# Attention over eight elements: scattered operand loads by groups of four heads, Q and K projected early, row maxima spread from the first score on

## The reference, cut to what matters

```
x: (8, 256, 512)   cond: (8, 512), zeros and ones
# layer 0: attention along the last axis, 16 heads of 16, masked
Q, K, V = W @ x[b]                         # 256x256 weights, 512 tokens
att = softmax((Q K^T / 4 + b0) * m + (1 - m) * -1e30)
x = x + (att V)^T
# layer 1: attention over 256 tokens, 16 heads of 32
xn = rms_norm(x) * g * (1 + scale) + shift # scale, shift from cond
q, k, v = xn @ W_qkv;  q, k = rms_norm(q), rms_norm(k)
o = softmax(q k^T / sqrt(32)) v
x = x + o + o @ W_out
# layer 2: a GRU over 256 steps.  layer 3: block attention and layer norm
```

## Time and profile before

| what | value |
|---|---|
| median of three runs | 2219.55 us |
| the profiled execution, its own time | 2220.39 us |
| its span in the trace | 2218.5 us |
| mean granted TensorE clock | 0.861 of full |
| busy: PE, DVE, ACT, POOL | 1912.1, 1271.6, 1088.1, 375.9 us |
| attention, until the GRU's first matmul | 0 to 1227.65 us |

### The profile page before, as it was taken

One profiled execution on the slowest core, in us unless ns is written; L12 is line 12 of the kernel. 1 busy time (PEld: TensorE's weight loads), 2 busy tenths in 40 slices (PEclk: granted clock), 3 DMA queues, 4 the chain that ended last, 5 costly groups with the idle time before them and its releaser, 6 DMA issues. The chain is left out here.

```text
span 2218.5 us, 87931 instructions
## 1 busy us (share of the span) xinstructions
PE 1912.1 (86%) x33566; PEld 1397.6 (63%) x33566; DVE 1271.6 (57%) x5543; ACT 1088.1 (49%) x4105; POOL 375.9 (17%) x1398
## 2 busy tenths in 40 slices
PE   5857978898788887898997899999999998989876
PEld 3224445363454544545463788888888898989775
DVE  4526346274462743636423477777777777777766
ACT  0332634635436354372653455555556565656444
POOL 3000000000000000000000133333333333343334
PEclk7678989999899999999998879897979797979557
DMA  8041233403333033331212300000000000000002
GB/s 222 6 65 40 61 49 81 68 11 86 54 81 62 9 94 54 81 54 15 72 63 57 101 1 1 0 0 0 0 0 0 0 0 0 0 0 0 0 0 76
DMA packets 100390, 86.87 MB, mean 39 GB/s; under 512 B 12472, under 2 KB 87352, under 8 KB 100296
## 3 DMA queue, kind: packets, MB, share of 16 engines
q1 hardware_dynamic: 99272, 85.41, 17.4%
q10 hardware_dynamic: 640, 0.13, 0.0%
q0 software_dynamic: 384, 0.01, 0.0%
HBM read 60.20 MB, written 21.00 MB: 37 GB/s over the span
## 5 line engine op out<-in xcount | busy, mean ns | idle before, releaser
L1202 PE MATMUL bank_pair_A<-moving,rep 128*128 128x16 f16 x8192 | 328.7, 172 | 69.4 <-ACT bank_pair_C L1285 40.6
L1202 PEld LDWEIGHTS bank_pair_A<-moving,rep 128*128 128x128 f16 x8192 | 268.2, 99 | 107.8 <-DVE moving L1427 81.0
L1202 PE MATMUL bank_pair_C<-moving,rep 128*128 128x16 f16 x8192 | 321.6, 171 | 0.0
L1202 PE MATMUL bank_pair_B<-moving,rep 128*128 128x16 f16 x8192 | 321.6, 171 | 0.0
L1202 PEld LDWEIGHTS bank_pair_B<-moving,rep 128*128 128x128 f16 x8192 | 266.2, 99 | 0.0
L1202 PEld LDWEIGHTS bank_pair_C<-moving,rep 128*128 128x128 f16 x8192 | 266.1, 99 | 0.0
L1294 ACT ACTIVATE r_gate<-r_pre 128x8 f32<-128x8 f32 (+1 forms) x512 | 110.3, 215 | 292.4 <-DVE r_pre L1387 255.2
L1189 PE MATMUL bank_pair_D<-x_part,w_in 128*128 128x256 f16 x1536 | 207.2, 282 | 6.1 <-ACT gi_rz L1322 3.5
L1082 POOL TENSOR_TENSOR x<-x,w_in 128x512 f32<-128x512 f32 x8 | 10.2, 1273 | 1077.8 <-DMA w_in<-w_in 1077.8
L547 PE MATMUL bank_pair_A<-rep 96*128 96x512 f16 x256 | 91.1, 443 | 108.0 <-DMA rep<-parts 65.3
L989 DVE TENSOR_REDUCE head_max<-bank_pair_A 128x2 f32<-128x1024 f32 x128 | 155.9, 1218 | 43.9 <-PE bank_pair_A L547 43.3
(11 more groups left out here) (250 smaller groups left out, 3570.4 us busy)
## 6 DMA issues: line engine op xcount, KB each, us to landing
rep<-parts SPq DMA_DIRECT2D x64, 256.0 KB, 10.9
parts<-parts SPq DMA_DIRECT2D x48, 256.0 KB, 2.1
q_rep<-parts SPq DMA_DIRECT2D x32, 256.0 KB, 4.9
k_rep<-parts SPq DMA_DIRECT2D x64, 128.0 KB, 2.8
w_in<-in_x_dram SPq DMA_DIRECT2D x8, 512.0 KB, 5.2
x<-in_x_dram SPq DMA_DIRECT2D x8, 512.0 KB, 4.4
w_in<-w_in SPq DMA_DIRECT2D x128, 32.0 KB, 2.0
parts<-parts SPq DMA_DIRECT2D x32, 128.0 KB, 2.7
```

The lines of the kernel that those rows point to most:

```text
L1202: last = nc.tensor.matmul(ps[part][:, o:o + 2 * B], w[:, k, (first + c) * P:(first + c) * P + P], moving[:, k, :, :].rearrange("p s b -> p ...
```

## The change

- `load_rep` takes a group of four heads: one DMA of mask rows and eight of 64 KB into the four heads' part of `rep`. The group of element b+1 waits for the last scores of the same group in attend(b), and not for all 32 units. The first maximum of each group waits for that group's loads.
- In attend, `q` moves to units 1 to 4, `k` to 7 to 10, `v0` to 27 to 30; `max1` moves to units 13 to 20 and `neg1`, `row1` to 22.
- Finish begins with a `max`, has one ahead of every `score1`, two behind every `res` and one behind each of the first `qk` chunks; `neg` follows the last of them and `row` the next chunk. Element 0's finish begins with six.
- SP's order: both stores of parts follow the loads of x and the mask; `load_rep` of groups 0 to 3 is placed among three `move_y`. The fourth `move_y` is issued by ACT, ahead of its steps of finish.
- `score1` of heads 0 and 1 share one bank of pair C (head 1 waits for head 0's exponent), then the two banks of pair C take turns.

The diff, cut:

```diff
-        score1_bank = [pA[:, 0, :], pA[:, 1, :], pB[:, 0, :], pB[:, 1, :]] + [pC[:, h % 2, :] for h in range(4, H)]
+        score1_bank = [pC[:, 0, :]] + [pC[:, (h + 1) % 2, :] for h in range(1, H)]
...
+            if b + 1 < B:
+                for n in range(NC * NC):
+                    at(1 + n, ("q", n))
+                at(5, ("q_split", 0))
+                for n in range(NC * NC):
+                    at(7 + n, ("k", n))
+                at(10, ("k_full", 0))
+                at(12, ("k_split", 0))
+                for n in range(DC):
+                    at(27 + n, ("v0", n))
             if b >= 1:
                 for h in range(H):
-                    at(3 + h // 2, ("max1", h))
-                at(11, ("neg1", 0), ("row1", 0))
-            if b + 1 < B:
-                for n in range(NC * NC):
-                    at(14 + n, ("q", n))
-                at(17, ("q_split", 0))
-                for n in range(NC * NC):
-                    at(20 + n, ("k", n))
-                at(23, ("k_full", 0))
-                at(25, ("k_split", 0))
-                for n in range(DC):
-                    at(26 + n, ("v0", n))
+                    at(13 + h // 2, ("max1", h))
+                at(22, ("neg1", 0), ("row1", 0))
...
             for h in range(H):
+                yield from maxes(1)
                 yield "score1", h
...
-                if h >= 8:
-                    yield from maxes(1)
...
+            yield from maxes(1)
             yield "inv1", G - 2
...
-            yield from maxes(1)
             for oc in range(DC):
                 yield "res", oc
-                yield from maxes(1)
+                yield from maxes(2)
                 if oc == 0:
                     yield "xnT", 0
             yield "xT", 0
-            yield from rest_order(free, 2)
+            yield from rest_order(free, 1)
 
         def first_order():
 
             free = iter(range(U0))
+            for u in islice(free, 6):
+                yield "max", u
             yield "x1", 0
             yield "rms", 0
-            yield "norm", 0
             for u in islice(free, 4):
                 yield "max", u
+            yield "norm", 0
             yield "tokens", 0
             yield "xnT", 0
             yield from rest_order(free, 3)
 
         def rest_order(free, per_chunk):
+            done = False
             for m in range(M8):
                 yield "qk", m
-                for u in islice(free, per_chunk):
-                    yield "max", u
+                some = [("max", u) for u in islice(free, per_chunk)]
+                yield from some
+                if some and some[-1][1] == U0 - 1:
+                    yield "neg", 0
+                    done = True
+                elif done:
+                    yield "row", 0
+                    done = False
             yield "qk", M8
-            left = list(free)
-            for u in left:
-                yield "max", u
-            if left:
-                yield "neg", 0
-            yield "v", 0
-            if left:
+            if done:
                 yield "row", 0
-            for n in range(1, DC * NC):
-                yield "v", n
+            yield from (("v", n) for n in range(DC * NC))
...
-            def load_rep(b):
-
+            def load_rep(b, g):
+
+                heads = slice(4 * g, 4 * g + 4)
                 if b >= 1:
-                    sp.wait_ge(st_ps, b * U0)
-                sp.dma_start(k_rep[64:67, :, :], mask_rows[b:b + 1, :, :].rearrange("o r t -> (o r) t").unsqueeze(1)
-                             .broadcast_to([3, H, D])).then_inc(ld_rows, 16)
+                    sp.wait_ge(st_ps, (b - 1) * U0 + 2 * DC * (g + 1))
+                sp.dma_start(k_rep[64:67, heads, :], mask_rows[b:b + 1, :, :].rearrange("o r t -> (o r) t").unsqueeze(1)
+                             .broadcast_to([3, 4, D])).then_inc(ld_rep[g], 16)
                 sp.wait_ge(st_parts, b * 64 + 64)
                 for rep0, rows in ((q_rep, ((0, 0), (0, 32), (1, 16), (1, 48))), (k_rep, ((2, 0), (2, 16), (3, 32), (3, 48)))):
                     for n, row in rows:
-                        sp.dma_start(rep0[row:row + DH0, :, :], parts0[n].rearrange("h d t -> d h t")).then_inc(ld_rep, 16)
-
+                        sp.dma_start(rep0[row:row + DH0, heads, :], parts0[n][heads, :, :].rearrange("h d t -> d h t")).then_inc(ld_rep[g], 16)
...
-                move_y(b, 0)
                 if more:
                     store_parts(b + 1, 0)
-                move_y(b, 1)
+                    store_parts(b + 1, 1)
+                for g in range(G - 1):
+                    if more and g >= 1:
+                        load_rep(b + 1, g)
+                    move_y(b, g)
+                    if more and g == 0:
+                        load_rep(b + 1, g)
                 if more:
-                    store_parts(b + 1, 1)
-                move_y(b, 2)
-                if more:
-                    load_rep(b + 1)
+                    load_rep(b + 1, G - 1)
                 else:
                     sp.wait_ge(st_ps, B * U0)
                     sp.dma_start(w_ih_f32, W_ih.rearrange("(c p) n -> p c n", p=P)).then_inc(w_ih_ld, 16)
-                move_y(b, 3)
                 spread1(b)
...
-                        pe.wait_ge(max1_ok, b - 1)
+                        pe.wait_ge(v1_ok, b - 1)
...
+                if tc == 0 and b >= 2:
+                    pe.wait_ge(max1_ok, b - 1)
...
-                if u == 0:
-                    pe.wait_ge(ld_rep, b * 128 + 128)
-                    pe.wait_ge(ld_rows, b * 16 + 16)
-                    pe.wait_ge(q_lo_ok, b + 1)
-                if u == 1:
-                    pe.wait_ge(kf_ok, b + 1)
+                if u % (2 * DC) == 0:
+                    pe.wait_ge(ld_rep[u // (2 * DC)], b * 144 + 144)
+                if b == 0 and u == 0:
+                    pe.wait_ge(q_lo_ok, 1)
+                if b == 0 and u == 1:
+                    pe.wait_ge(kf_ok, 1)
                 if u < 2:
-                    if b >= 2:
-                        pe.wait_ge(exp1_ok, (b - 2) * H + 2 * u + 2)
-                    elif b == 1:
-                        pe.wait_ge(exp_ok, U0)
+                    if b >= 1:
+                        pe.wait_ge(exp_ok, b * U0 - 1 + u)
                 else:
                     pe.wait_ge(s_max, b * U0 + (u - 1))
...
                 if h == 0:
                     pe.wait_ge(max1_ok, e + 1)
-                if e + 1 < B:
-                    if h in (0, 2):
-                        pe.wait_ge(exp_ok, (e + 2) * U0 - 1 + h // 2)
-                    if h in (4, 5):
-                        pe.wait_ge(y_ok, (e + 1) * G + (h - 1))
-                elif h == 4:
-                    pe.wait_ge(qn_ok, e * M8 + M8)
-                if h >= 6:
+                if h == 0:
+                    if e + 1 < B:
+                        pe.wait_ge(y_ok, (e + 1) * G + 3)
+                    else:
+                        pe.wait_ge(qn_ok, e * M8 + M8)
+                elif h == 1:
+                    pe.wait_ge(exp1_ok, e * H + 1)
+                elif h == 2 and e + 1 < B:
+                    pe.wait_ge(y_ok, (e + 1) * G + 4)
+                elif h >= 3:
                     pe.wait_ge(exp1_ok, e * H + (h - 1))
...
+            def move_last_y(b):
+
+                g = G - 1
+                act.wait_ge(y_ok, b * G + G)
+                for j in range(4):
+                    r = (4 * g + j) * DH0
+                    act.dma_start(y[r % P:r % P + DH0, r // P, :], y_pad[g % 2][32 * j:32 * j + DH0, :]).then_inc(ld_y[g % 2], 16)
...
                 if b + 1 < B:
                     v_part(b + 1)
+                move_last_y(b)
                 steps(BESIDE[b], b, b - 1)
```

More of the change, by code:

```diff
@@ L250, in _ @@
                 last.then_inc(c_condt, 1)
-        ld_x1, ld_mask, ld_rows, st_parts, ld_rep, ld_max = (
-            sem(n) for n in ("ld_x1", "ld_mask", "ld_rows", "st_parts", "ld_rep", "ld_max"))
+        ld_x1, ld_mask, st_parts, ld_max = (sem(n) for n in ("ld_x1", "ld_mask", "st_parts", "ld_max"))
+        ld_rep = [sem(f"ld_rep_g{g}") for g in range(G)]
         ld_y = [sem(f"ld_y{n}") for n in range(2)]
@@ L408, in _, with move_y @@
         def _(sp):
+            def move_y(b, g):
+                sp.wait_ge(y_ok, b * G + g + 1)
+                for j in range(4):
+                    r = (4 * g + j) * DH0
+                    sp.dma_start(y[r % P:r % P + DH0, r // P, :], y_pad[g % 2][32 * j:32 * j + DH0, :]).then_inc(ld_y[g % 2], 16)
             def load_x(b):
@@ L427, in store_parts @@
                 if b >= 1:
-                    sp.wait_ge(ld_rep, b * 128)
+                    for g in range(G):
+                        sp.wait_ge(ld_rep[g], b * 144)
                 for n, ready in ((0, q_hi_ok), (1, q_lo_ok)) if which == 0 else ((2, k_hi_ok), (3, k_lo_ok)):
@@ L472, in _ @@
             store_parts(0, 1)
-            load_rep(0)
+            for g in range(G):
+                load_rep(0, g)
```

(2 more changed lines are left out.)

## The result

| | before | after |
|---|---|---|
| median, us | 2219.55 (2216.96 to 2224.35, 11 runs) | 2227.04 (2221.09 to 2232.15, 11 runs) |
| the profiled execution, its own time / span | 2220.39 / 2218.5 | 2232.15 / 2230.3 |

The ratio is 1.003, with a 95% interval of 1.0018 to 1.0041: slightly slower, where 2180 was forecast. The profiled execution lies 5.1 above its median. Part of that can be its launch: its first maximum comes at 35.95, and in eight other profiled executions with the same start (experiments 1 to 3, 5 to 7, 9 and 10) it comes at 32.7 to 33.5 in five and at 35.4 to 35.9 in three. Against the profiled execution of before, the first eight matmuls of the Q projection ran at half clock (6.67 us for the group that took 3.67 there) and began 0.8 later.

What follows compares the result with a forecast made beforehand. Attend was taken as bound by PE, finish by waits for `rep` and DVE's maxima. Terms -12.5 - 18.4 - 71.1 + 7.3 + 54 + 1.2 = -39.5 took 2220.4 to 2180.9, so 2180; range 2148 to 2214.

Steps and rivals of the forecast that it cites:

- the wait for x: At attend's Q projection: x lands at A (start of the next attend) + 10.8, so PE stands about 10 us.
- The issues on ACT: At finish's start: ACT's four DMAs for the last `y` take 2.4 us ahead of its first exponent.
- PE's restart: After the second `score1`'s wait: PE restarts about T (end of attend's last `pv`) + 6.1; half clock adds 1.7.
- the `qk` chunks: In finish: chunks fall from 3.5 to 2.6 and 2.2 us; first `qk` to A takes 30.2.
- x does stop PE: Denies the rival of no stop: `spread1` pieces keep pace with PE, 61 us stay saved, 2119; chance 0.07.
- ACT's issues: Rival at finish's start: the four issues take 7.4, 5 us more in seven finishes, 2215; chance 0.07.
- the last of them: Rival: group loads wait in SP's queue, PE still waits 7.9 for `rep`, about 2227; chance 0.05.
- clock rival: Rival: clock stays at half through finish's `score1` stretch, 12 us an element, +72, 2252; chance 0.07.
- Attend becomes 10.8 + (49.6 - 0.9) + 0.2 for `q_split` ... + 2.5: Attends 2 to 6: x's landing, PE's remaining work, `q_split` and clock restart make 62.2, 10.8 more each.
- 15.8 ... 2.2 ... 1.7 ... T + 25.8 at the third `weigh1`: Finish's score stretch: 14 maxima 15.8, DVE's other steps 2.2, half-clock restart 1.7; third `weigh1` at T + 25.8.
- First maximum near 31: Kernel start: only a quarter of `rep`'s bytes is needed, first maximum at 31.3, saving 12.5 us.
- Element 7 and lone +1.2: Last element: ACT's issues against an unqueued `y` cost 0.5, `lone_order` pays 0.7 for the shared bank.

Runs made afterwards that it cites:

- experiment 1: Changed kernel with x and mask loads of element b + 2 issued ahead of `spread1(b)`; 2159.13 us, ratio 0.9727 to the kernel before.
- experiment 2: Changed kernel with the last `y` moved by SP behind the fourth group's loads, no DMA on ACT; 2197.49 us, ratio 0.9898 to the kernel before.
- experiment 3: Changed kernel with `max1` from unit 15 instead of 13 and its `neg1`, `row1` at 24; 2206.7 us, ratio 0.994 to the kernel before.
- experiment 5: Changed kernel with early x, last `y` by SP, `max1` from 15 with `row1` at 24, `q_split` at 4; 2111.52 us, ratio 0.9503.
- experiment 6: Changed kernel with every group's `rep` load waiting for all 32 units and behind three `move_y`; 2225.06 us, ratio 1.0023 to the kernel before.
- experiment 7: Kernel of experiment 5 with the `rep` loads behind attend's last scores, last `y` behind them on SP; 2174.34 us, ratio 0.9785 to the kernel before.
- experiment 9: Changed kernel with `q_split` at unit 4 instead of 5, nothing else; 2212.45 us, ratio 0.9965 to the kernel before.
- experiment 10: Changed kernel with `q_split` at 4 instead of 5 and `k_split` at 11 instead of 12; 2200.63 us, ratio 0.989 to the kernel before.
- experiment 4: Kernel before with x and mask loads issued early, ahead of `spread1`; 2223.54 us, ratio 1.0006.
- experiment 8: Kernel before with only the change's new attend order and both stores ahead of the `y` moves; 2257.15 us, ratio 1.0162.

## Why the prediction was wrong

**Right.** The mechanism of the wait for x and its size: 9.0 to 10.1 at the projection's matmul in attends 2 to 6 (line 514 in the kernel before, 519 in the changed one), "near 10" foretold, and `q` beginning at A + 10.0 to 11.1 where 10.8 was said. Its price by experiment 1, which takes it out of after and leaves the two small waits, is 67.45 - 54.80 = 12.65 an attend; the sum had 12.4 (10.8 less 0.9 of work, and 2.5 for the restart). The issues on ACT: 2.46 for four (2.4 said), PE's restart at T + 6.18 (6.1 said), and with three to four heads at half clock behind it 4.08 in all by experiment 2, where 2.4 and 1.7 were counted. PE does not wait for `rep` in finish, and the `qk` chunks are at 2.6 and 2.2: 30.55 from the first to A, 30.2 said. From the third `weigh1` to the first `res` 8.0, as said. None of the four rivals held: x does stop PE, the clock comes back at 577.4 in the score stretch, ACT's issues took 2.46 and not 7.4, and no wait for `rep` was left. That the time came out at the 2227 of the last of them is chance. (The clock rival's own sum gives 12.7 an element and 2256, not 12 and 2252.)

The Trainium skill's "DMA: Bandwidth & Descriptors" (Anatomy of one DMA), whose fit for another issuing path makes 3.2 of this load by the prediction's estimate, does not describe it here: `q` began 5.4 behind the issue of x.

**Wrong**, 51.3 us of the profiled spans (11.8 against -39.5):

- **"Attend becomes 10.8 + (49.6 - 0.9) + 0.2 for `q_split` ... + 2.5"** is the step that failed: 26.1 in attends 2 to 6 and 3.0 in attend 1. Measured, an attend of after is 67.45 in the mean, not 62.2. By the runs it is made of 51.56 (experiment 5, no wait over 0.7 left), 3.24 for the two small waits (experiment 1, which has them and no wait for x: 54.80 - 51.56) and 12.65 for x on top of them. Against the sum, 5.25 an attend:
  - 2.0: PE's busy time, 49.6, was taken as the length of attend without waits. The 1.8 idle of the earlier trace rows was thought to vanish into the wait for x. It does not; it lies in many small gaps behind it.
  - 3.0: `q_split` was priced at 0.2 and `max1` at nothing. The text said of each moved step what it issues, but not what stands in line behind its last part: ACT's high part of Q lies one exponent later, and K's first matmul waits 1.16 for DVE's low part; K's low part lies ahead of the first maxima of layer 1, and PE waits 2.26 and 0.2. Experiments 3, 9 and 10 show both.
  - 0.25 for x, 12.65 against 12.4. In it lies a second stretch at half clock: the wait of 2.26 is followed by half rate in attends 2 to 6 of after and in none of experiment 1. Without that wait x costs 12.0 (experiment 10 less 5, with 10's wait of 0.92 in it), which would leave some 0.65 for the second stretch. That a wait of 2.3 could bring half clock was not considered.
- **"15.8 ... 2.2 ... 1.7 ... T + 25.8 at the third `weigh1`"**: it came at T + 26.9. With 0.35 an element in the chunks and small differences between the elements the six finishes are 8.25 over the sum. DVE was taken to be busy throughout; in element 3 it stands 0.68 and 0.16 for PE behind the first two `weigh1` steps, which keep PE from the next pair.
- **"First maximum near 31", -12.5**: it came at 35.95, and at 32.7 to 35.9 in the other profiled executions of this start. The old start scatters as well: 43.79, 44.4 and 47.0 (before, experiments 4 and 8). So how much of the 4.7 missed is the launch and how much the sum stays open.
- **"Element 7 and lone +1.2"**: +7.3. PE waits 5.87 there for ACT (3.6 more from T to the first `qk`); experiment 2 takes 4.7 of it back. Of the other 3.6, 1.8 lies between that `qk` and the GRU's first matmul: 80.34, where it is 78.4 to 78.7 with the old banks (before, experiments 4 and 8) and 79.6 to 80.3 in all kernels with the new ones, 1.1 to 1.8 for the shared bank and what follows it where 0.7 was said. The last 1.8 is in the GRU and behind it, where no step was changed.
- Element 0: its attend was set to 0. It has the wait of 1.16 too, and is 2.0 longer. Its finish gave 16.8 of the 18.4; the first `qk` was at T + 20.0 (19.6 said).

The chances: 0.84 on faster rested on one case whose parts were each taken singly. For attend the range allowed 3 us in the landing of x and nothing else. The two small waits alone (3.0 in six attends) are 18, the idle time in attend (2.0 in six) 12 and the finishes 8: 2218 together, beyond the upper end of 2214.

**What became of the gain.** The finishes did give back 62.9 and element 0's 16.8. Attends 1 to 6 took 90.4 for it. The early group loads, which were to remove the wait for `rep`, removed one that ACT's issues put back in the same place (experiment 6). With x loaded earlier, the last `y` issued by SP, `q_split` one unit earlier and `max1` two units later, the same change is worth 5% (experiment 5).

## What to carry to other kernels

When a step is moved forward, follow every engine that takes part in it up to its last piece, and ask on each what now stands behind that piece: here ACT's high part behind an exponent and DVE's low part ahead of other maxima cost 3.2 us an attend together, a quarter of what the large wait cost. When one stretch gets faster, look for a chain beside it that does not (SP's stores and loads of the pieces), and put the loads that the next stretch needs first ahead of that chain. And look twice before an engine that computes on the critical path (ACT here) issues DMAs there: four held it for 2.46 us, and cost 4.1 with the clock behind them.

## What was not expected of the hardware

**A wait of some 2.2 us is followed by half clock in one place and not in another.** Two kernels, both with PE's wait of 2.17 at the second `score1`: in experiment 2, at element 3, the matmuls behind it take full rate; in experiment 5 they do not.

```profile
557.53 0.28 PE L670 MATMUL bank_pair_C<-q_rep,k_rep 128*128 128x256 f16 x1 [2.17 <-ACT probs L866]
```
```profile
556.00:559.00 3.00, 1.47 (x14) 1.04 (x14) 2.90 (x4) 2.07 (x4) 0.00 (x0) 1.00 0.28 79
```
```profile
515.50:519.00 3.50, 3.36 (x17) 2.09 (x18) 2.90 (x3) 1.26 (x3) 0.00 (x0) 0.52 0.28 74
```

The first two rows are of experiment 2, the third of experiment 5. In experiment 2 the six finishes alternate for it: 43.48 or 43.49 from T to the first `qk` where full rate follows, and 44.14 or 44.15 in the other three. The wait of 2.26 ahead of `max1` likewise: 0.52 for 3.4 us behind it in after, and 1.00 as the mean of the whole attend in experiment 1. In experiment 9 both happen in one kernel, behind the waits of elements 2 and 3:

```profile
475.05:529.85 54.80, 50.55 (x451) 23.15 (x449) 17.83 (x33) 38.15 (x42) 1.27 (x1) 1.00 0.30 87
```
```profile
381.50:385.00 3.50, 3.41 (x34) 1.75 (x34) 3.04 (x5) 1.17 (x2) 0.00 (x0) 1.00 0.26 75
526.40:530.00 3.60, 3.57 (x20) 1.44 (x20) 2.38 (x5) 0.35 (x1) 0.00 (x0) 0.54 0.26 87
```

The first row is experiment 1, the other two experiment 9. Behind the five waits of 9 to 10 for x and the six of 4.7 to 4.9 for ACT in after the rate was half each time. What was waited for does not settle it: the short waits for x in experiment 8 (1.8 to 2.5, a DMA) are followed by full rate in all five attends, here behind the one of 2.20:

```profile
533.77:538.77 5.00, 5.00 (x31) 2.02 (x32) 0.00 (x0) 2.05 (x2) 0.00 (x0) 1.00 0.00 1
```

The Trainium skill, "TensorE: Matmul & The Clock Gate" (HAM oscillation), tells of another kernel, whose waits on DMA between bursts, longer than the short ones here, brought the half rate back every time. For the waits of 9 to 10 on DMA the trace agrees; for the short ones nothing came back, and there the measurement decides.

In element 0's finish seven waits of 1.8 to 2.2 follow one another 6 to 8 us apart, and which of them is followed by half rate differs between kernels. Two neighbours in after, then two neighbours in experiment 9 (each row is one pair of scores, 1.03 or 1.04 long at half rate, 0.59 or 0.60 at full):

```profile
168.11 1.03 PE L552 MATMUL bank_pair_A<-rep 96*128 96x512 f16 x2 [2.13 <-DVE head_max L1007]
175.44 0.60 PE L552 MATMUL bank_pair_B<-rep 96*128 96x512 f16 x2 [2.13 <-DVE head_max L1007]
```
```profile
177.57 0.59 PE L552 MATMUL bank_pair_A<-rep 96*128 96x512 f16 x2 [2.23 <-DVE head_max L1007]
185.01 1.04 PE L552 MATMUL bank_pair_B<-rep 96*128 96x512 f16 x2 [2.14 <-DVE head_max L1007]
```

The stretch from the first `qk` to A takes 61.8 in after and 59.5 in experiment 9. It is not scatter of single executions: it takes 59.5 to 60.0 in the four kernels with `q_split` at unit 4 (experiments 5, 7, 9 and 10) and 61.7 to 63.4 in the five others of the new order, whatever their launch was. No step in the stretch differs between them. That it depends on when the waits fall is the likeliest reading, not shown by a run made for it. It would mean that such a kernel moves by a few microseconds when something ahead of its waits is shifted. Of the 14.6 of experiment 9, 8 to 10 were to come from the waits that it removed, and the rest lies, as far as the rows show, where half rate no longer came: here, and behind some of the waits ahead of `max1`.
